# Two passes of a segment attention, head h and head h+1, written into the engines' queues in alternating pieces

## The reference

```python
x = x + attn_a(layernorm(x))        # full softmax attention, one head of 1024
x = x + ffn(layernorm(x))           # token shift, sigmoid gate, relu squared
x = x + attn_b(layernorm(x))        # below
x = x + ffn(layernorm(x))
```

```python
def step(carry, seg):               # 4 segments of 512 tokens, 8 heads of 128
    M, z = carry
    qs, ks_, vs = seg
    sq = elu(qs) + 1.0
    sk = elu(ks_) + 1.0
    a_mem = (sq @ M) / (sq @ z + EPS)
    v_delta = vs - (sk @ M) / (sk @ z + EPS)
    M_new = M + sk.T @ v_delta
    z_new = z + sk.sum(axis=2)
    scores = where(causal_mask, qs @ ks_.T / sqrt(128), min)
    a_dot = softmax(scores) @ vs
    return (M_new, z_new), gate * a_mem + (1.0 - gate) * a_dot
```

## Time and profile before

| | |
|---|---|
| two runs | 9646.74 and 9836.17 us, median 9741.45 |
| profiled execution | 9616.6 us |
| its span on the slowest core (core 2) | 9614.9 us |
| spans of the 8 cores | 9592.8 to 9614.9 us |
| mean granted TensorE clock, core 2 | 0.722 |
| busy: PE, DVE, ACT | 5115.5 us (53%), 2916.5 us (30%), 2920.1 us (30%) |
| chain that ended last, by engine | PE 46%, DVE 17%, ACT 15%, DMA 11%, issue 10% |

### The profile page before, as it was taken

One profiled execution on the slowest core, in us unless ns is written; L12 is line 12 of the kernel. 1 busy time (PEld: TensorE's weight loads), 2 busy tenths in 40 slices (PEclk: granted clock), 3 DMA queues, 4 the chain that ended last, 5 costly groups with the idle time before them and its releaser, 6 DMA issues.

```text
span 9614.9 us, 81914 instructions; the slowest of 8 cores (9592.8 to 9614.9 us)
## 1 busy us (share of the span) xinstructions
PE 5115.5 (53%) x26688; PEld 2458.6 (26%) x26688; DVE 2916.5 (30%) x6569; ACT 2920.1 (30%) x5666; POOL 8.6 (0%) x14
## 2 busy tenths in 40 slices
PE   3866344435586644443558664444355866444437
PEld 1323122212232312221223231222122323222213
DVE  1124233343112423334311242333431124233343
ACT  3222333331322233333132223333313222333331
POOL 0000000000000000000000000000000000000000
PEclk9988665557798865555779886655577988655558
DMA  2010100001101010000110101000111010100010
GB/s 71 18 35 8 45 1 1 25 29 48 57 18 35 3 50 1 1 22 31 44 62 18 35 1 53 1 1 18 35 40 66 18 35 1 53 1 1 18 35 35
DMA packets 69436, 256.95 MB, mean 27 GB/s; under 512 B 7584, under 2 KB 7584, under 8 KB 69024
## 3 DMA queue, kind: packets, MB, share of 16 engines
q1 hardware_dynamic: 50592, 184.60, 5.7%
q10 hardware_dynamic: 18432, 67.12, 2.1%
HBM read 218.14 MB, written 33.55 MB: 26 GB/s over the span
## 4 chain that ended last, share of the span: by engine, by line
PE 46%; DVE 17%; ACT 15%; DMA 11%; issue 10%; DVEq 1%; ACTq 0%; SPq 0%
PE pb L170 36%; PE pb L183 6%; DVE a L699 4%; ACT ptbuf L938 2%; PE pb L949 2%; ACT warena L305 2%; DMA x_tm<-x 2%; ACT ebuf L909 2%; DVE xn_tm L1057 2%; DVE a L1004 2%; DVE a L692 1%; DMA out<-x_tm 1%; ACT xn_fm L460 1%; ACT xn_tm L1001 1%; DVE ebuf L923 1%
## 5 line engine op out<-in xcount | busy, mean ns | idle before, releaser
L170 PE MATMUL pb<-a,warena 128*128 128x512 bf16 x6144 | 1435.5, 395 | 348.0 <-DVE a L699 155.9
L170 PE MATMUL pb<-xn_fm,warena 128*128 128x512 bf16 x5120 | 1171.7, 393 | 78.2 <-ACT xn_fm L460 51.7
L170 PEld LDWEIGHTS pb<-a,warena 128*128 128x128 bf16 x6144 | 612.1, 101 | 1150.1 <-issue 509.3
L351 ACT ACTIVATE junkb<-x_tm 128x1024 bf16<-128x1024 f32 x256 | 270.4, 1056 | 1920.7 <-DMA x_tm<-x 682.3
L183 PE MATMUL pb<-identb,xn_tm 128*128 128x128 bf16 x2304 | 242.3, 280 | 1080.5 <-ACT xn_tm L415 761.3
L170 PE MATMUL pb<-ebuf,warena 128*128 128x512 bf16 x2048 | 516.4, 417 | 421.2 <-DVE a L763 394.4
L170 PEld LDWEIGHTS pb<-xn_fm,warena 128*128 128x128 bf16 x5120 | 511.4, 101 | 726.2 <-issue 167.0
L183 PE MATMUL pb<-identb,ebuf 128*128 128x128 bf16 x2304 | 286.3, 261 | 726.3 <-DVE ebuf L923 726.3
L170 PE MATMUL pb<-a 128*128 128x128 bf16 (+4 forms) x2560 | 479.3, 277 | 62.5 <-DVE xn_tm L1015 62.4
L170 PE MATMUL pb<-xn_tm,ptbuf 128*128 128x512 bf16 x2048 | 469.4, 383 | 69.6 <-DVE ptbuf L580 69.6
L183 PEld LDWEIGHTS pb<-identb,xn_tm 128*128 128x128 bf16 x2304 | 199.4, 127 | 1131.4 <-issue 1128.5
(11 more groups left out here) (104 smaller groups left out, 5307.0 us busy)
## 6 DMA issues: line engine op xcount, KB each, us to landing
out<-x_tm SPq DMA_DIRECT2D x64, 512.0 KB, 2.6
warena<-wkfT ACTq DMA_DIRECT2D x48, 512.0 KB, 3.3
warena<-wrT SPq DMA_DIRECT2D x48, 512.0 KB, 3.5
warena<-wvfT SPq DMA_DIRECT2D x48, 512.0 KB, 3.3
x_tm<-x SPq DMA_DIRECT2D x48, 512.0 KB, 3.3
warena<-wqaT SPq DMA_DIRECT2D x24, 512.0 KB, 4.2
warena<-wkaT ACTq DMA_DIRECT2D x24, 512.0 KB, 3.4
warena<-wqb SPq DMA_DIRECT2D x24, 512.0 KB, 4.5
```

The source lines that it names most:

```text
L170: return e.matmul(out, lhsT, rhs, start=st, stop=sp)
L351: s2m = ac(lambda e, i=i: e.activation(out=junkb.ap(), in_=x_tm[:, i, :], func=AF.Square, accum_out=stats[:, i, 1:2]), waits=w + buf_war.g ...
```

## The change

Both passes become generators: `passA_g` yields after each `lc`, `passB_g` after Relu, Exp and max-add (L1005 of the kernel after), after copy and sum, after the denominators, and after each `lc`. The loop runs `passB_g(h)` and `passA_g(h+1)` in turns, one piece of each, `passB` first, until both are done. Everything else is as it was: the operations, their tiles, banks and waits.

```diff
-                def passA(h):
+                def passA_g(h):
...
                         buf_war["ptbuf"] = [adm]
+                        yield
...
-                def passB(h):
+                def passB_g(h):
...
                     el_m = [el, el]
+                    yield
...
                         op=ALU.add), waits=[el_m[1]], tag=f"{tag}zt{G}_{h}")
+                    yield
...
                         waits=[rbm], tag=f"{tag}gq{G}_{h}")
+                    yield
...
                         bank_war[nb] = c1_last
+                        yield
...
-                passA(0)
+                for _ in passA_g(0):
+                    pass
                 for h in range(H):
                     wstep()
+                    gens = [passB_g(h)]
                     if h + 1 < H:
-                        passA(h + 1)
-                    passB(h)
+                        gens.append(passA_g(h + 1))
+                    while gens:
+                        for g_ in list(gens):
+                            try:
+                                next(g_)
+                            except StopIteration:
+                                gens.remove(g_)
```

## The result

The kernel after takes 9617.87 us (median of 11 runs, 9439.33 to 9870.40), beside 9803.69 us (median of 10) for the kernel before on the same chip; the ratio is 0.984 with a 95% interval of 0.978 to 0.990. The forecast was 9420 us with a range up to 9600: the direction is right, the size is not, and the gain of 1.6% lies under the 2% that I had made likely (the interval, 1.0 to 2.2%, leaves both open). The profiled execution takes 9442.25 us against 9616.6, so 174 us less, where 242 were forecast.

The account below looks back on a forecast made before the run. The head loop was taken as bound by hand-over latency; -284 us in segments 1 to 3 and +42 in the fourth make -242, so 9616.6 becomes 9375, forecast as 9420 us with the offset of timed runs; range 9290 to 9600.

Parts of the forecast that it names:

- What bounds the loop: Head loop of the segment attention: latency of hand-overs, nearly always exactly one engine working; busy times make 23.66 us.
- The cycle, 19.9 us: Head loop with both passes in turns: new cycle P of 19.9 us, 3.66 less than 23.56.
- Rival 2: Hand-overs between the passes cost more, P between 20.4 and 22.5: gain under 192 us, time 9554; chance 0.17.
- Segments 1 to 3, -284 us: Head loops of the first three segments of each sequence: 150.45 against 174.13 us each, -284 us in 12 segments.
- The fourth segments, +42 us: Last segment of each sequence: weight casts now on the path, 200.5 against 189.90 us, four times making +42.
- Everything else, 0 us: Code outside the head loops: unchanged, as no instruction is added or removed and no tile or bank is new.
- the -242: All head loops together: the sum of -284 and +42 us, applied to the profiled execution's 9616.6 us.
- The offset: Whole kernel: timed runs lie 30 and 220 us above the profiled execution; from 9375 the forecast took 9420.
- The clock, 0.50: PE in the head loop: granted clock stays at 0.50, with PE busy 7.4 in 19.9 us.
- Rival 1: Head loop: the denser loop raises PE's clock, 146 us less, time 9274; chance 0.07.
- Rivals 3 and 4: Strict queues serialize both passes, casts laid bare: 9830 us, chance 0.06; ACT's waits on PE's counter: 9662 us, chance 0.03.
- the tail of `passB`: End of each head's cycle: `passB`'s last 3 us run beside the scaling and the next Relu and Exp, hidden.

Follow-up runs that it names:

- e5: Kernel after with 336 always-fulfilled waits added at the head of PE's and of DVE's instructions each; ratio 0.969 (0.963 to 0.974).
- e3: Kernel after without the last yield of `passA`, so sums and scaling stand ahead of that round's piece of `passB`; ratio 0.964 (0.960 to 0.969).
- e8: Kernel after with `wkfT` loads from SP, loader steps spread over rounds, `passA` yielding behind each Exp, turns from a list; ratio 0.943, lowest time 9047 us.
- e4: Kernel after without alternation: only Relu, Exp and maximum of `passB(h)` early, then all of `passA(h+1)`, then the rest of `passB(h)`; lowest time 9371 us.
- e7: Kernel after with `wkfT` loads issued from SP and one loader step per round instead of three at the cycle's head; lowest time 9235 us.
- e9: e8 with 336 always-fulfilled waits at the head of PE's instructions and 340 at the head of DVE's; lowest time 8988 us.
- e2: Kernel after, unchanged, timed again in another session beside the kernel before; ratio 0.982 (0.974 to 0.989).

## Why the prediction was right in mechanism and wrong in size

- **What bounds the loop.** Right, but one reading behind it is wrong. That the busy times of the three engines add up to the cycle does not mean that nearly always exactly one works: in the stretch of the earlier trace rows one engine is busy in 16.2 of 23.6 us, none in 3.7 and two in 3.7. It is by chance that overlap and idle hand-overs are of one size. After the change (1165.03 to 1185.11) none is busy in 2.7 of 20.1 us, and two or three are in 5.1. The rows show hand-overs throughout, and every reordering that took one off the path moved the cycle (23.6, 19.8, 18.5, 17.9) while the busy times of PE, DVE and ACT in a full cycle stayed within 0.35 us of the earlier trace rows.
- **The cycle, 19.9 us.** Right, at 19.79. The single steps hold: from the Relu to L1005 2.32 (2.33), to L923 3.47 (3.5), to the 256-column product 5.09 (5.14), to the first L1061 12.13 (12.21), to the next scaling 18.77 (18.9). So the `skt` transposes cost about what I gave them, 0.42 for 0.38, and the copy and the reduction are hidden, though with nothing to spare: the reduction ends at 1152.69 and the mask behind it starts at 1152.71. Rival 2 did not come. Its size did, 186 us between the medians where it had under 192, but by another cause, so the chance that I gave it for that is not borne out.
- **Segments 1 to 3, -284 us.** Right; -298 on core 1. The first segment takes 150.0 against 150.45 forecast. The rest is mostly that I took all twelve of before to be like the first at 174.1, while they average 175.0.
- **The fourth segments, +42 us.** Right in mechanism, at +52 on core 1. A segment takes 202.4 to 203.7 against 200.5. The later landing is in it: the wait for `wkfT` is 2.35 us at head 0 where the earlier trace rows had 1.93. With the landing as before (e5) the four are 789 to 794, which is +31 in the median. So the sum was 11 us too high for the order alone, and the landing added some 16 in the mean, 23 on core 1.
- **Everything else, 0 us.** This is the step that failed. The sum said "No instruction is added or removed, no tile or bank is new", and applied the -242 to the rest unchanged; the description of the change says too that all waits are as they were. The operations are, the waits are not: 672 went on PE and DVE and 80 came on ACT, and with the shorter lists the loads landed later. Outside the loops the kernel after lost 78 us on core 1 (32.3 + 59.3 - 12.4 - 1.5), 51 in the mean of the cores. e5 shows that the lists' length is the cause by putting it right. With the right landing the parts add up to -298 in the twelve loops, +31 in the four and -13 in the gaps between segments (for which I have no account), together -280; between the lowest times of e5 and of the kernel before on its chip are 279 us (9328 and 9607). The -242 was thus too small a gain for the order alone, and the -174 of the profiled execution is what the landing left of it.
- **The offset.** This term was mis-sized, and it is the larger part of the miss. Of the 198 us between 9420 and the median of 9618, 67 are the sum's (9375 against 9442), and 131 the offset's: I took 45 us, and the median of 11 lies 176 us above the profiled execution. Either alone would have stayed under 9600 (9442 + 45 = 9487, 9375 + 176 = 9551), both together did not. The median before is 187 above its own profiled execution, so both are lifted alike, which is why the ratio and not the median tells the size.
- **The clock, 0.50.** Right; PE is busy 7.06 of 20.08 us and granted 0.50. Rival 1 did not come, and no denser order brought it, down to 7.11 us of 18.00. The rule of the Trainium skill that stood behind it (TensorE: Matmul & The Clock Gate, section What's actually happening) says that the slow state is the default and activity releases it; this loop stayed in that state throughout, so no run of it shows the release.
- **Rivals 3 and 4.** ACT does not wait for PE's counter: L998 follows the scaling after 1.02 us with no wait before it, as in the kernel before. The wait that was new is at the scaling and for DVE's sums, 2.64 us. Rival 3's laying bare of the casts came, as part of the forecast; its price on P did not.

That I called the tail of `passB` hidden was right for this change (L1005 of the next head still waits for ACT, not for DVE's queue), and it is 0.5 us of the cycle in the next ones (e3, e8).

## What to carry to other kernels

In a loop bound by hand-overs between engines with in-order queues, look first for the one long chain that can start early (here Relu and Exp, e4), then put the sums that the next stage waits for ahead of foreign work on their queue (e3), and spread side work such as weight casts over the gaps (e7) instead of leaving it at a place that was a gap only in the old order. When a reordering gives less than its loop's cycle promises, cut both traces into stages and look at the code that was not touched: the number of instructions and the landing times of equal DMAs are two rows on the page that tell whether it still runs as before. A few hundred fulfilled waits are a cheap try when it doesn't. And a forecast of a median needs the spread between executions as a term of its own, here the larger error of the two.

## What the runs showed of the hardware that was not expected

- The landing of the same 512 KB loads depends on the length of the instruction lists of PE and DVE, between 3.3 and 3.95 us: lists 336 shorter each 3.63 on even and 3.83 on odd cores, 168 or 112 shorter each 3.70 and 3.95, one list 336 shorter 3.58 and some 3.72, equal to before or 336 longer 3.29 to 3.39. It does not change when the padding moves from the head to the tail. Kernels with lists of one length landed alike on whichever chip they ran, and late and early landing were both seen on each of four chips. The time goes between the first and the last packet of a load (2.0 us before, 2.3 to 2.7 where it is late), not between issue and first packet (0.93 to 0.96).
- Its price here, each lowest time taken against the kernel before on the same chip, is 66 us between e8 (-559) and e9 (-625), and 80 between e2 (-199) and e5 (-279), less than 1%, but as large as the differences one tunes for at this stage, and without a row of its own in the busy times.
- The clock stayed at its lower level, 0.50, in every order of the head loop, with PE busy from 7.37 of 23.60 us to 7.11 of 18.00 us.
